# C repeated into all partitions by DMA through device memory instead of by TensorE, two banks for the down projection, and reordered engine lists

## The reference

```python
x = x + 0.5 * ffn(layernorm(x))          # "A": gate, up, silu, quantize, down
x = x + ssm(layernorm(x))                # "S"
x = x + 0.5 * ffn(layernorm(x))          # "C"

def ssm(x):                              # N = 16 state entries, DM = 256 features
    BC = x @ W_in + b_in
    Bm, Cm = BC[..., :N], BC[..., N:]
    dt = clip(softplus((x @ W_dt1 + b_dt1) @ W_dt2 + b_dt2), 1e-07, 1e6)
    tmp = A * dt[..., None]
    A_bar = exp(tmp)
    B_barX = expm1(tmp) / tmp * dt[..., None] * Bm[:, :, None, :] * x[..., None]
    h = scan over the tokens of h[l] = A_bar[l] * h[l-1] + B_barX[l]
    return sum(h * Cm[:, :, None, :], axis=-1) + D * x
```

## Time and profile before

| | |
|---|---|
| Median of 3 runs | 3735.4 us (3733.07 to 3741.8) |
| The profiled execution's own time | 3751.63 us |
| Its span | 3749.5 us |
| Busy share of the span: PE, DVE, ACT, POOL | 88%, 91%, 80%, 77% |
| Mean granted TensorE clock | 0.964 |
| DMA queue q1, share of 16 engines | 24.0% |

### The profile page before, as it was taken

How to read it: one execution, slowest core, us unless ns; L and a number is a source line. 1 busy time by engine, 2 the same in 40 slices (tenths; PEclk the granted TensorE clock), 3 DMA queues, 4 the chain that set the end, 5 groups by cost and what they waited for, 6 DMA issues and landing times. The chain is left out here.

```text
span 3749.5 us, 79627 instructions
## 1 busy us (share of the span) xinstructions
PE 3298.2 (88%) x28716; PEld 2354.3 (63%) x28716; DVE 3407.0 (91%) x5419; ACT 2999.4 (80%) x6314; POOL 2871.2 (77%) x2489
## 2 busy tenths in 40 slices
PE   0479999999999999999999999999999999999984
PEld 0256666666666666666666666666666666666663
DVE  6389999999999999999999999999999999999984
ACT  1278888888888888888888888888888888888872
POOL 1457788888878788888788888778888887888854
PEclk9789999999999999999999999999999999999987
DMA  1112222222322222222222223222322222222212
GB/s 31 28 35 49 45 55 53 63 46 55 63 47 52 53 63 46 55 60 51 47 57 63 46 55 63 45 50 58 52 53 59 49 55 52 60 58 47 53 35 42
DMA packets 583023, 192.07 MB, mean 51 GB/s; under 512 B 544039, under 2 KB 578280, under 8 KB 582632
## 3 DMA queue, kind: packets, MB, share of 16 engines
q1 hardware_dynamic: 582632, 186.98, 24.0%
HBM read 19.16 MB, written 16.78 MB: 10 GB/s over the span
## 5 line engine op out<-in xcount | busy, mean ns | idle before, releaser
L917 DVE TENSOR_TENSOR_SCAN state<-w_ps,decay 128x512 f32<-128x512 f32 x1024 | 1208.9, 1206 | 63.0 <-PE w_ps L1299 60.9
L1225 PE MATMUL gu_ps<-wgu,qxT 128*128 128x352 f16 x6144 | 1035.3, 320 | 135.3 <-DMA qxT<-qx 55.8
L1299 PE MATMUL w_ps<-bdif,x_parts 128*128 128x129 f16 (+1 forms) x12288 | 852.4, 222 | 94.9 <-DVE state L917 87.9
L1225 PEld LDWEIGHTS gu_ps<-wgu,qxT 128*128 128x128 f16 x6144 | 577.4, 100 | 516.7 <-issue 93.5
L1299 PEld LDWEIGHTS w_ps<-bdif,x_parts 128*128 128x128 f16 x12288 | 756.3, 99 | 217.0 <-issue 174.0
L1119 ACT ACTIVATE decay<-dt,A_sb 128x512 f32<-128x512 f32 x1024 | 686.1, 711 | 74.3 <-DVE state L917 41.9
L927 DVE SCALAR_TENSOR_TENSOR c_state<-state,inv_A,rep_ps 128x512 f32<-128x512 f32 x1024 | 721.3, 734 | 9.1 <-issue 3.8
L506 POOL TENSOR_TENSOR bdif<-dif,B_lo 128x516 f16<-128x516 f16 x512 | 536.2, 1060 | 167.8 <-PE w_ps L1299 166.8
L1319 PE MATMUL y_ps<-ident,c_state 128*128 128x128 f32 x4352 | 621.6, 279 | 27.0 <-DVE c_state L927 26.9
L1239 PE MATMUL dn_ps<-wd,qhT 128*128 128x256 f16 (+1 forms) x4608 | 590.3, 278 | 62.4 <-DMA qhT<-qh 60.8
L1107 ACT ACTIVATE bdif<-dif,B_tok 128x129 f16<-128x129 f16 x2048 | 628.9, 393 | 0.0
(11 more groups left out here) (160 smaller groups left out, 3805.9 us busy)
## 6 DMA issues: line engine op xcount, KB each, us to landing
x_in<-in_L_attn_x SPq DMA_DIRECT2D x32, 512.0 KB, 3.8
x_s<-x_a SPq DMA_DIRECT2D x32, 512.0 KB, 3.8
out<-x_out SPq DMA_DIRECT2D x32, 512.0 KB, 3.2
qhT<-qh SPq DMA_TRANSPOSE x256, 3.7
qxT<-qx SPq DMA_TRANSPOSE x128, 3.1
hid<-in_L_ffn_w_gate SPq DMA_DIRECT2D x1, 704.0 KB
bdif<-in_L_ffn_w_up SPq DMA_DIRECT2D x1, 704.0 KB
val<-in_L_ffn_w_down SPq DMA_DIRECT2D x1, 704.0 KB, 13.5
```

Source lines behind the costliest of these rows:

```text
L917: v.tensor_tensor_scan(state[:, n % 2, gi, :], w_ps[:, gi, :], decay[:, n % 2, gi, :], 0.0, ALU.add, ALU.mult).then_inc(state_ready.sem, 1)
L1225: last = te.matmul(gu_ps[:, m, 0:FH], qxT[:, t // 2, 4 * (t % 2) + xp * G + c], wgu[:, c, wp, a:a + FH], start=begin, stop=end)
L1299: last = te.matmul(w_ps[:, gi, t * P:t * P + wide], x_parts[:, seq % 2, xp, t, gi * P:(gi + 1) * P], bdif[:, n % NB, t, bp, 0:wide], start ...
```

## The change

Four things are changed.

1. C is no longer repeated by PE. After `take_rBC` has written `rBC`, SP copies its 16 rows of C (`rBC[ROW_C:PR]`, 16 x 512 f32, 32 KB) to the scratch `C_rows` in device memory (`keep_C`, step `cw`). Then eight DMAs (`repeat_C`, steps `cr0` to `cr7`) each read two rows (4 KB) for every partition and write them to the SBUF tile `C_all` [128, 16, 512] f32, 512 KB each. `times_c` now reads `C_all[:, n, :]` in place of `rep_ps`. `repeat_c`, `high_C`, `low_C`, `pick_row`, `C_parts`, `rep_ps` and their semaphores are gone.
2. `dn_ps` has two banks, used in turn; `down` waits for the residual addition two before it.
3. `take_rBC` waits for the C_rows copy of the sequence before; `repeat_C` waits for the `c_state` of the sequence before that used these rows.
4. The five lists in `ORDER` are rewritten.

The diff, cut to its core (of the lists only a few lines):

```diff
 ORDER = {
     "DVE": """
...
-    S.p22 S.p23 R.tb0 N.xs0 C.qm3 C.qv2 R.sc0 R.cb0 S.p24 S.g26 S.g27 S.p25 S.g28 S.p26 S.p27 C.qv3 N.xm0 N.xm1
...
+    C.qm3 S.p23 C.res0 C.res1 R.tb0 S.g26 S.p24 S.g27 S.g28 R.cb0 S.p25 S.p26 S.p27 N.xm0 C.qv3 S.g29 S.p28
...
     "SP": """
-    S.keep0 C.tx0 C.tx1 A.ht0 A.ht1 A.ht2 A.ht3 N.load0 C.ht0 C.ht1 C.ht2 C.ht3 N.tx0 N.tx1 C.store0
+    C.tx0 S.keep0 C.tx1 S.cr5 A.ht0 A.ht1 S.cr6 S.cr7 A.ht2 A.ht3 C.ht0 N.load0 C.ht1 C.ht2 R.cw0 C.ht3 N.tx0
+    N.tx1 C.store0 R.cr0 R.cr1 R.cr2 R.cr3 R.cr4
     """,
 }
...
-        dn_ps = psum("dn_ps", [P, DM])
+        dn_ps = psum("dn_ps", [P, 2, 512])
         y_ps = psum("y_ps", [P, G, L])
         w_ps = psum("w_ps", [P, 2, L])
-        rep_ps = psum("rep_ps", [P, L])
...
-        C_parts = sb("C_parts", [P, 2, L], F16)
+        C_all = sb("C_all", [P, N, L])
+        C_rows = nc.dram_tensor("C_rows", [2, N, L], F32, kind="Internal").ap()
...
+            def keep_C(seq):
+
+                sp.wait_ge(r_ready.sem, r_ready.at(seq, 1))
+                if before(seq, 2):
+                    for k in range(N // 2):
+                        sp.wait_ge(C_in[k].sem, C_in[k].at(seq - 2, 16))
+                sp.dma_start(C_rows[seq % 2], rBC[ROW_C:PR, :]).then_inc(C_out.sem, 16)
+
+            def repeat_C(seq, k):
+
+                sp.wait_ge(C_out.sem, C_out.at(seq, 16))
+                if not first(seq):
+                    sp.wait_ge(c_state_ready.sem, c_state_ready.at(seq - 1, G + 2 * G * k + 2 * G))
+                sp.dma_start(C_all[:, 2 * k:2 * k + 2, :],
+                             C_rows[seq % 2, 2 * k:2 * k + 2, :].unsqueeze(0).broadcast_to([P, 2, L])
+                             ).then_inc(C_in[k].sem, 16)
...
                 if gi == 0:
-                    dve.wait_ge(rep_full.sem, rep_full.at(seq, n + 1))
+                    dve.wait_ge(C_in[n // 2].sem, C_in[n // 2].at(seq, 16))
                 dve.wait_ge(state_ready.sem, state_ready.at(seq, m + 1))
-                v.scalar_tensor_tensor(c_state[:, n % 2, gi, :], state[:, n % 2, gi, :], inv_A[:, gi, n:n + 1], rep_ps[:],
+                v.scalar_tensor_tensor(c_state[:, n % 2, gi, :], state[:, n % 2, gi, :], inv_A[:, gi, n:n + 1], C_all[:, n, :],
                                        ALU.mult, ALU.mult).then_inc(c_state_ready.sem, 1)
...
             def take_rBC(seq):
                 act.wait_ge(rB_ps.sem, rB_ps.at(seq, 1))
+                if not first(seq):
+                    act.wait_ge(C_out.sem, C_out.at(seq - 1, 16))
                 a.activation(rBC[:], gu_ps[0:PR, 0, :], ACT.Identity, bias=b_rBC[0:PR, :]).then_inc(r_ready.sem, 1)
...
-                if t:
-                    pe.wait_ge(ffn_done.sem, ffn_done.at(q, t))
+                if t >= 2:
+                    pe.wait_ge(ffn_done.sem, ffn_done.at(q, t - 1))
                 elif not first(q):
-                    pe.wait_ge(ffn_done.sem, ffn_done.at(q - 1, T))
+                    pe.wait_ge(ffn_done.sem, ffn_done.at(q - 1, T + t - 1))
...
-            def repeat_c(seq, n):
-                if n:
-                    pe.wait_ge(c_state_ready.sem, c_state_ready.at(seq, G + G * n))
-                else:
-                    pe.wait_ge(C_lo.sem, C_lo.at(seq, 1))
-                te.matmul(rep_ps[:], pick_row[:, n, :], C_parts[0:KC, seq % 2, :], start=True, stop=True).then_inc(rep_full.sem, 1)
```

More of the change, by code:

```diff
@@ L28 @@
     "PE": """
[L29 to L33, removed]
@@ L35 @@
+    C.dn1 R.bt0 S.w26 S.w27 C.dn2 S.w28 S.p22 S.p23 S.w29 S.w30 R.z0 S.p24 S.p25 S.p26 S.p27 S.w31 S.p28 C.dn3
+    S.p29 S.p30 S.p31
     """,
     "DVE": """
[L37 to L40, removed]
@@ L298, in macaron_program @@
         r_ready = count("r_ready", 1)
-        C_hi = count("C_hi", 1)
-        C_lo = count("C_lo", 1)
         B_ps = count("B_ps", 1)
@@ L308, in macaron_program @@
         dt_ready = count("dt_ready", G + 1)
-        rep_full = count("rep_full", N)
+        C_out = count("C_out", 16)
+        C_in = [count("C_in_%d" % k, 16) for k in range(N // 2)]
         b_hi_ready = count("b_hi_ready", N)
@@ L371, in _ @@
             sp.dma_start(b_rBC[ROW_C:PR, :], column(b_in[N:2 * N])).then_inc(bc_in.sem, 16)
[L372 to L373 removed]
+            sp.dma_start(b_C[ROW_B:ROW_B + N, :], column(b_in[N:2 * N])).then_inc(bc_in.sem, 16)
             sp.dma_start(W_dt2_sb[:], W_dt2).then_inc(consts_in.sem, 16)
@@ L420, in body @@
                 for stage, step, k in pieces:
-                    if step == "tx":
+                    if step == "cw":
+                        keep_C(it)
+                    elif step == "cr" and stage == "R":
+                        repeat_C(it, k)
+                    elif step == "cr":
+                        repeat_C(it - 1, k)
+                    elif step == "tx":
                         turn_x(q[stage], k)
@@ L862, in ffn_residual @@
                 dve.wait_ge(dn_ready.sem, dn_ready.at(q, t + 1))
-                v.scalar_tensor_tensor(dst[:, t, :], dn_ps[:], down_back[:, 0:1], src[:, t, :], ALU.mult, ALU.add,
+                v.scalar_tensor_tensor(dst[:, t, :], dn_ps[:, t % 2, 0:DM], down_back[:, 0:1], src[:, t, :], ALU.mult, ALU.add,
                                        accum_out=None if sums is None else sums[:, t:t + 1]).then_inc(ffn_done.sem, 1)
@@ L883, in times_B @@
                                        rBC[ROW_B:ROW_B + N, :], ALU.add, ALU.mult).then_inc(CB_ready.sem, 1)
-            def low_C(seq):
-                dve.wait_ge(r_ready.sem, r_ready.at(seq, 1))
-                dve.wait_ge(C_hi.sem, C_hi.at(seq, 1))
-                if before(seq, 2):
-                    dve.wait_ge(rep_full.sem, rep_full.at(seq - 2, N))
-                v.scalar_tensor_tensor(C_parts[2 * N:KC, seq % 2, :], gu_ps[ROW_C:PR, 0, :], b_C[0:N, :],
-                                       C_parts[0:N, seq % 2, :], ALU.add, ALU.subtract).then_inc(C_lo.sem, 1)
             def make_dt(seq):
@@ L950, in body @@
                         times_B(it)
-                    elif step == "sc":
-                        low_C(it)
                     elif step == "k":
@@ L1064, in take_rBC @@
                 act.wait_ge(rB_ps.sem, rB_ps.at(seq, 1))
+                if not first(seq):
+                    act.wait_ge(C_out.sem, C_out.at(seq - 1, 16))
                 a.activation(rBC[:], gu_ps[0:PR, 0, :], ACT.Identity, bias=b_rBC[0:PR, :]).then_inc(r_ready.sem, 1)
-            def high_C(seq):
-                act.wait_ge(rB_ps.sem, rB_ps.at(seq, 1))
-                if before(seq, 2):
-                    act.wait_ge(rep_full.sem, rep_full.at(seq - 2, N))
-                a.activation(C_parts[0:N, seq % 2, :], gu_ps[ROW_C:PR, 0, :], ACT.Identity,
-                             bias=b_C[0:N, :]).then_inc(C_hi.sem, 1)
             def softplus(seq):
@@ L1147, in body @@
                         take_rBC(it)
-                    elif step == "ch":
-                        high_C(it)
                     elif step == "xh":
@@ L1238, in down @@
                         begin, end = (c, hp, wp) == (0, 0, 0), (c, hp) == (FC - 1, 1)
-                        last = te.matmul(dn_ps[:], qhT[0:k, t % 2, hp * FC + c, :], wd[0:k, c, wp, :], start=begin,
+                        last = te.matmul(dn_ps[:, t % 2, 0:DM], qhT[0:k, t % 2, hp * FC + c, :], wd[0:k, c, wp, :], start=begin,
                                          stop=end)
@@ L1339, in body @@
                         differences(seq, k)
-                    elif step == "c":
-                        repeat_c(seq, k)
                     elif step == "e":
```

61 lines of the change are left out of this document (29 added, 32 removed).

## The result

The changed kernel takes 4075.7 us (median of 4 runs, 4069.5 to 4083.0), the kernel before in the same comparison 3734.2. The ratio is 1.0895, 95% interval 1.0863 to 1.0926: slower, by 341 us, against the 403 of the sum. The prediction was 4137.

The account below looks back on a forecast made before the run. DVE was taken to set the turn. Stall +15.2, own duration -1.0, `low_C` -0.75, PE relief -2.5 and POOL +2 gave +13 us a turn, +403 over 31 turns; scaled to the median, 4137 us, range 3880 to 4480.

Parts of the forecast that it names:

- Rival 1: `c_state` with both tensors in SBUF isn't blocked by POOL, so the kernel gets faster: 3620 us, chance 9%.
- rival 3: Repeats into `C_all` are slow because 128 partitions read the same 4 KB; at 20 us each near 6200 us, chance 4%.
- Rival 2: `c_state` blocks, but its waits fall into DVE's idle time or POOL's pauses: 3735 to 3850 us, chance 5%.
- The stall, +15.2 a turn: On DVE, the 32 `c_state` a turn wait for POOL's instructions: +15.2 us a turn, bounds 11.8 to 28.
- The formula: Stall on DVE: each run of `c_state` waits 0.41 us, each follower directly behind another 0.98; 25 runs, 7 followers.
- The reordered lists get no term of their own beyond the runs counted: The new engine orders were given no cost or gain except through the count of `c_state` runs and followers.
- Its own duration, -1.0: `c_state` itself shorter with both inputs in SBUF, priced from L696: -1.0 us a turn; the skill's fixed costs gave -2.1.
- PE's relief, -2.5: Without `repeat_c` PE's results come earlier and DVE waits less for PE: -2.5 us a turn, from nothing to -5.8.
- POOL pushed, +2: POOL instructions wait behind `c_state`, so their values return later to DVE: +2 us a turn, from nothing to +7.
- The DMAs, 0: The nine added DMAs on SP, eight copies at 3.8 us each, stay hidden within the turn: 0.
- The worry about `cr0`: The first repeat DMA lands only 1 to 2 us before its reader; if that cover is gone, a us a turn.
- Worth at most 0.9 a turn: The second PSUM bank for `down` saves at most DVE's wait for `dn_ps`, 0.9 us a turn.

Follow-up runs that it names:

- e3: The kernel before with `c_state` reading a constant SBUF tile in place of `rep_ps`, C left out, repeats and lists kept: 4325.1 us, ratio 1.1566.
- e5: The changed kernel with the lists of before (removed steps dropped) except SP's new list, nothing left out: 4312.1 us, ratio 1.1505.
- m1: A separate kernel running `c_state`'s instruction alone and beside POOL: both tensors in SBUF 1972 ns beside reading POOL, 744 beside POOL only writing, 747 alone.
- e4: The changed kernel with `C_all` set once, without the DMAs to and from `C_rows` and their waits, C left out: 4077.3 us, ratio 1.0892.
- e7: The kernel before with `rep_ps` set once, without PE's 512 repeat matmuls and the waits for them, C left out: 3732.0 us, ratio 0.9955.
- e8: e5 with `c_state` made by a reduction that reads `state` alone, C and 1/A left out: 3759.8 us, ratio 1.0036.
- e6: The changed kernel with `c_state` made by a reduction that reads `state` alone, C and 1/A left out: 3925.2 us, ratio 1.0475.

## Why the prediction was right, and where its terms were off

**Direction and mechanism: right.** `c_state` with two SBUF tensors is blocked by POOL's reading; e3 shows that this alone slows the kernel, e5 does the same with C in place, and m1 isolates it. Rival 1 (nothing blocks) falls with the mean of 992 ns, rival 3 (slow repeats) with e4. Rival 2 has more truth than its 5% gave it: the waits do fall partly where POOL stands still, though not enough for its 3735 to 3850.

**The stall, +15.2 a turn: too large; measured +8.84, with the own duration (-1.0) inside.** The formula fits an order that wasn't made for it. Applied to the old list, with 20 runs and 12 followers, it gives 20 x 0.41 + 12 x 0.98 = 20.0, in a turn of 109.6 + 578 / 31 = 128.2 us 17.1; e5 measures 32 x (1279 - 734) = 17.4 by the mean durations, e3 17.0. For the new list it gives 15.2, and 32 x (992 - 734) = 8.3 were measured in the same way. The step that failed is "The reordered lists get no term of their own beyond the runs counted". Of the 632 `c_state` that stand alone in the changed kernel's timeline, 208 begin while POOL is idle and take 0.74 us, the other 424 take 1.16, 0.42 more; in e5, 97 of 264 and 1.40. So one that stands alone doesn't meet a standing POOL more often than in the old lists (33% against 37%), but where it meets a busy one it waits 0.42 us in place of 0.66. Those in pairs and threes wait 0.24 us each and not 0.41 and 0.98, as at 2114.79 us above; in e5 each of a pair waits about 0.6.

**Its own duration, -1.0: wrong, though small.** It came from the slope of another instruction in the earlier trace rows. m1 has 747 ns for two SBUF tensors and 743 with one in PSUM: nothing. The estimate of -2.1 from the Trainium skill ("VectorE: DVE Perf Modes", The TRN2 errata) has no support in these two rows either. The measured durations decide.

**PE's relief, -2.5: wrong.** By e7 it is 9 / 31 = 0.3 us a turn (0.1 to 1.0 by the interval), in the old lists, and in the changed kernel DVE's idle time rose from 5.8 to 6.9. The three waits of DVE for PE in the earlier trace rows, 171.7 us over the whole span, are still 154.3 in e7, so they were not there because PE had too much work in total. That they come from where single steps stand is the likely reading, not a shown one.

**POOL pushed, +2: too large, and by another way.** L524 (L506 before) stayed at 1062 ns, and L563 (L545 before) grew by 163 ns. What came back on DVE is `magic` and `qh`, +1.65 together, less 0.76 in `qx`: about +0.9.

**The DMAs, 0: right** (e4). The worry about `cr0` was sound, but for the old order without blocking: e8, where the first `c_state` stands in its old place, waits for `C_all` 67.2 us, 2.2 a turn, near the microsecond or two of cover that the prediction counted. In the changed kernel no `c_state` waits for `C_all`.

**The lists' own price and the second bank: missing.** The lists cost 165 us by e6 and e8, some 5 us a turn. In the sum this missing term, and the relief that was counted and did not come, stand against a stall that was too dear by about 6.5 us a turn. That the total, 403 against 341, is nearer than its parts is luck: errors of opposite sign cancelled. "Worth at most 0.9 a turn" for the bank was read from waits in the old order; for the new one it was 396 / 31 = 13.

Of the signs that were named: the minimum (651 ns), the maximum (2007), DVE's share (91%), PE's share (9 points less), the queue's share (+6.1 points) and the missing wait for `C_all` came as said; the mean of `c_state` (992 ns, not 1.1 to 1.3 us), DVE's busy time (+290 us, not over 400) and the longer L506 and L568 (+3 and +37 ns, not 0.1 to 0.3 us) did not, and neither did a POOL instruction between two adjacent `c_state` (inside 2 of some 180 groups). L545 did get longer as said.

**What stays open.** Which of the moved steps make up the 165 us was not tried apart. The new lists with the repeats on PE need a ninth PSUM bank and weren't tried. `state` written to PSUM by the scan would spare `c_state` the stall, by m1's L95, but needs four banks for its four buffers; that wasn't tried either. Of all kernels with C in place the one before is the fastest.

## What to carry to other kernels

Before an operand is moved from PSUM to SBUF, look at the other operand of its DVE instruction and at what POOL reads at that time: here a free-looking move cost 595 us by itself. Such a stall has no fixed price; here it was about the time from the instruction's start to the end of POOL's present one, so it is changed by the order, and an order that suits the stalled kernel can lose time in one without a stall (-236 and +165 us). A buffer's worth, too, belongs to an order: read from the old one it was nothing, under the new one 396 us.
